# Layer 0's self attention: VectorE's order of minima and reciprocals, and its share of the copies of turned probabilities

## The reference

```python
scores = jnp.einsum('bhqd,bhkd->bhqk', Q, K) / dk ** 0.5
scores = jnp.where(causal, scores, -jnp.inf)
probs = jax.nn.softmax(scores, axis=-1)
attn = jnp.einsum('bhqk,bhkd->bhqd', probs, V)
```

## Time and profile before

| | |
|---|---|
| median of three runs | 858.41 us |
| the profiled execution | 859.32 us |
| its span | 857.4 us |
| TensorE busy | 767.4 us, 90% |
| VectorE busy | 612.8 us, 71% |
| ScalarE busy | 455.8 us, 53% |
| GpSimd busy | 432.6 us, 50% |
| L836 exponentials, ScalarE | 88.3 us busy, 192 instructions |
| L922 normalisation, GpSimd | 82.0 us busy, 80 instructions |
| L678 copies of turned probabilities, VectorE | 28.7 us busy, 48 instructions |

### The profile page before, as it was taken

The page is one execution under the profiler, slowest core; times in us unless marked ns, Lnnn a source line. Parts: engine busy times, 40 slices in busy tenths (PEclk is TensorE's granted clock), DMA queues, the critical chain, the costliest instruction groups (busy, mean ns, idle before and its releaser), DMA issues. The chain is left out here.

```text
span 857.4 us, 18273 instructions
## 1 busy us (share of the span) xinstructions
PE 767.4 (90%) x5842; PEld 483.8 (56%) x5842; DVE 612.8 (71%) x2052; ACT 455.8 (53%) x1447; POOL 432.6 (50%) x428
## 2 busy tenths in 40 slices
PE   6999989897959999999999999999894699999943
PEld 3766666665834444555555555787674555555523
DVE  1666777796856777898888888342345778888956
ACT  2387787673431001888888888100333087777724
POOL 4355565562004666766666666000630478888840
PEclk9999999999979999999999999999996599999977
DMA  9400000000004666300000000240378222222225
GB/s 323 189 2 2 2 2 1 2 1 1 1 14 101 166 171 152 99 2 2 1 1 1 2 1 1 109 206 18 107 260 211 104 63 76 75 79 72 73 64 190
DMA packets 32237, 63.17 MB, mean 74 GB/s; under 512 B 6592, under 2 KB 21068, under 8 KB 31280
## 3 DMA queue, kind: packets, MB, share of 16 engines
q1 hardware_dynamic: 20704, 41.40, 15.1%
q0 software_dynamic: 4896, 11.95, 4.5%
q10 hardware_dynamic: 6544, 8.67, 3.8%
HBM read 41.01 MB, written 9.84 MB: 59 GB/s over the span
## 5 line engine op out<-in xcount | busy, mean ns | idle before, releaser
L1418 ACT ACTIVATE a_room<-a_room,a_nm 128x257 f32<-128x257 f32 x256 | 127.3, 499 | 100.6 <-DVE a_nm L1261 99.8
L1460 POOL TENSOR_TENSOR a_room<-a_room,a_rd 128x1024 f32<-128x1024 f32 x64 | 121.3, 1895 | 65.8 <-DVE a_rd L1269 65.4
L1261 DVE CUSTOM_DVE_ANT_0 a_room<-a_ps,table,NSK 128x256 f32<-128x256 f32 x256 | 107.8, 478 | 0.4 <-PE a_ps L1120 0.4
L836 ACT ACTIVATE l_Pr<-l_Sm,l_nm 128x128 f32<-128x128 f32 (+1 forms) x192 | 88.3, 461 | 32.9 <-DVE l_nm L656 18.9
L922 POOL TENSOR_TENSOR l_Pr<-l_Pr,l_rd 128x256 f32<-128x256 f32 (+1 forms) x80 | 82.0, 1043 | 46.7 <-DVE l_rd L670 46.5
L1120 PEld LDWEIGHTS a_ps<-room 64*128 64x128 f32 x512 | 44.1, 186 | 53.2 <-issue 48.5
L1120 PE MATMUL a_ps<-room 64*128 64x256 f32 x512 | 72.3, 402 | 0.5 <-DVE a_nm L1261 0.5
L1200 PE MATMUL a_ps<-a_room,W 128*128 128x512 f32 x160 | 71.2, 602 | 0.8 <-ACT a_room L1432 0.8
L1241 DVE SCALAR_TENSOR_TENSOR a_room<-a_ps,BQK,table 128x512 f32<-128x512 f32 x80 | 56.4, 746 | 20.6 <-PE a_ps L1200 20.6
L1135 PE MATMUL a_ps<-table,a_room 128*128 128x128 f32 x512 | 69.7, 279 | 1.1 <-ACT a_room L1427 1.1
L1148 PE MATMUL a_psO<-a_room,room 128*64 128x512 f32 x256 | 68.8, 617 | 0.0
(11 more groups left out here) (323 smaller groups left out, 1780.6 us busy)
## 6 DMA issues: line engine op xcount, KB each, us to landing
room<-a_room SPq DMA_DIRECT2D x96, 64.0 KB, 2.0
room<-a_room ACTq DMA_DIRECT2D x96, 64.0 KB, 2.1
room<-in_w_in SPq DMA_DIRECT2D x1, 6144.0 KB, 18.3
room<-in_c_in SPq DMA_DIRECT2D x1, 4096.0 KB, 15.3
room<-pairs SPq DMA_DIRECT2D x8, 512.0 KB, 8.0
W<-in_w SPq DMA_DIRECT2D x1, 3072.0 KB, 12.4
room<-in_w_out SPq DMA_DIRECT2D x1, 3072.0 KB, 20.0
W<-in_wo SPq DMA_DIRECT2D x1, 2048.0 KB, 8.4
```

What stands on the lines that cost most here:

```text
L836: nc.scalar.activation(Pr[:, t % 4, n, 0:n_keys], Sm[:, t % 2, n, 0:n_keys], ACT.Exp, bias=nm[:, t % 2, n:n + 1], scale=-1.0, accum_out=de ...
L1261: nc.vector.tensor_tensor_reduce(out=Sm[:, t % 2, n, 0:S], in0=psS(t)[:, n // 2, n % 2, :], in1=c["window"][:, n % 2, :], scale=-1.0, scal ...
L1418: nc.scalar.activation(Pr[:, t % 4, n, :], Sm[:, t % 2, n, :], ACT.Exp, bias=nm[:, t % 2, n:n + 1], scale=-1.0, accum_out=den[:, t % 2, n: ...
L1460: pool.tensor_tensor(p, p, rd[:, t % 2, :].unsqueeze(2).to_broadcast([P, 4, S]), ALU.mult).then_inc(normed, 1)
```

## The change

In self slots VectorE now issues peak(t) before invert(t-1), as it did in cross slots. In odd self slots (16 of them) VectorE copies both banks of turned probabilities, one behind the other, after its single wait for both halves of the turn; ScalarE has no copy in these slots. The first of the two copies counts up `copied_a`, the second `copied_v`. The number and size of all copies stay the same. Cross slots and the rest of the program are not edited.

```diff
     def kind(self, t):
         return self.groups[t // 2][0]
+
+    def both_by_vector(self, t):
+        return self.kind(t) == "self" and t % 2 == 1
 
                 w = plan.width(t)
+                if plan.both_by_vector(t):
+                    nc.vector.tensor_copy(PT[:, i % 2, 2 * (t % 2), 0:w], psT[:, 0, 0:w]).then_inc(s["copied_a"], 1)
                 nc.vector.tensor_copy(PT[:, i % 2, 2 * (t % 2) + 1, 0:w], psT[:, 1, 0:w]).then_inc(s["copied_v"], 1)
 
             for t in range(steps):
-                if t < slots and plan.kind(t) == "cross":
+                if t < slots:
                     peak(t)
                 if 0 <= t - 1 < slots:
                     invert(t - 1)
-                if t < slots and plan.kind(t) == "self":
-                    peak(t)
 
                 if t < slots:
                     exps(t)
-                if 0 <= t - LT < slots:
+                if 0 <= t - LT < slots and not plan.both_by_vector(t - LT):
                     keep(t - LT)
```

## The result

The changed kernel takes 868.95 us (median of four runs, 866.44 to 872.1) against 858.58 (four runs of the kernel before): ratio 1.0102, interval 1.0078 to 1.0125. Slower, as forecast, but by 10.4 us between the medians and 8.7 between the profiled executions instead of 4.3, and outside the range (858.8 to 865.2). The profiled execution took 868.06 with a span of 866.3; before's span was 857.4, so 8.9 us are to be found.

A forecast was written before the change was run, and what follows sets the result against it. TensorE was taken to bound layer 0's attention. Batch terms +1.36, +1.13, +1.0 and +0.8 sum to +4.3 us on the profiled 859.32, giving 863.6, less 0.9 for the median: 862.7 us; 8-in-10 range 858.8 to 865.2.

The forecast's parts named there:

- The new ring from odd turn to odd turn: Layer 0 self slots: turn, two copies, minima, reciprocal, normalisation, next odd turn take 5.29 us; TensorE needs 4.93.
- +1.36 in the first batch: Layer 0, first batch: turn(2) at 55.06, then odd turns 5.29 apart bring turn(10) to 75.86 instead of 74.50.
- +0.70 at turn(13): Layer 0, behind the first output: double copy and later minima(14) put turn(13) at 87.06 instead of 86.36.
- The sign the prediction named: Start of layer 0's cross attention: the first cross score comes 3.5 to 4.3 us later than before.
- The delay stays: Behind layer 0: each stage takes its input from the last, so the +4.3 us reach the end unchanged.
- With the new order alone every ring would be of 4.81: Layer 0 self slots: with one copy per slot, rings take 4.81 us, below TensorE's 4.93 for two slots.
- TensorE's rate: Rival, layer 0 self slots: two slots stay at 4.93 us and only the cover moves; 857.8 us, chance 0.13.
- ScalarE's relief: Rival, layer 0 behind outputs: fewer ScalarE copies shorten the recovery; 853.1 us at best, 855 likelier, chance 0.05.
- the dearer pair: Rival, odd self slots: second copy held to the first's end, ring 5.45 us; 864.3 to 866 us, chance 0.14.
- No later stage took the delay in: Rival, stages behind layer 0: a wait ending at a fixed time absorbs the delay; 858.5 to 860 us, chance 0.06.

The follow-up runs named there:

- order_odd_steps: The changed kernel, but in even self steps the reciprocal stands ahead of the minima again; ratio 1.012 (1.008 to 1.016) to the kernel before.
- the badly filled one: The changed kernel with three extra matmuls in each of TensorE's two waits behind an output, which stood behind ScalarE's copy and waited 2.39 us; ratio 1.025.

## Why the prediction was right or wrong

- *The new ring from odd turn to odd turn, 5.29*: right, measured 5.21; every link within 0.05 of its row. The last was 0.05, not 0.10, and the pair of copies 0.94, not 0.96. order_odd_steps shows that the minima in it make the difference.
- *+1.36 in the first batch*: 1.1 (first scores to output 35.52 against 34.43), as three passes through the ring at 0.08 less give. The odd turns wait 0.22 for GpSimd, not 0.3 to 0.4.
- *Behind the outputs +0.70 at turn(13)*: 0.62 counted from the output (87.56 less 77.37 is 10.19, before 9.57), of which the wait before score 16 has 0.38 and that before turn 13 0.24. Both items over all batches: forecast 3.9 to the first cross scores, measured 3.1. Right in mechanism, 0.8 too much. The sign the prediction named, the first cross score 3.5 to 4.3 later, came at 3.1.
- *"The delay stays: behind layer 0 every stage takes its input from the last"*: this step failed. It let the delay pass through unchanged and so put the change of TensorE's clock at nothing; the earlier trace rows gave 1.00 and no reason why that should last. The runs showed half clock behind the longer waits, and later stages met more of it too: +6.3 us from the first cross scores on, where the forecast added about 0.4. Some 4.8 of these are the three further stretches at half clock. The same omission is in "With the new order alone every ring would be of 4.81", taken as harmless: the order alone, with 0.24 more of waiting in one place per batch, cost 0.9%.
- *The rivals*: TensorE's rate did not hold, ScalarE's relief gained nothing, and the second copy was not held to the end of the first (0.48 after 0.56), so the dearer pair is out as well. No later stage took the delay in. None of them named the clock. That the change would be slower was forecast from a mechanism that the trace shows; its size was not.
- *Supported by runs, not settled*, that two waits behind an output bring half clock when they are long enough: it shows between 43 and 155 us in all seven profiles in which both are there and add up to 1.33 us or more. These are the changed kernel three times and four others; the badly filled one is left aside. It shows in none of the eight in which they add up to 1.18 or one of them is gone or filled. By places, it followed 12 of the 21 outputs in the seven profiles and none of the 24 in the eight. So a longer wait makes it likely and not certain. The two sums were found after the runs and nothing between them was measured. Why the clock also falls in the feed-forward stays open: a stretch at half clock stands there (between 208 and 236 us) in 11 of the 14 profiles of kernels other than the one before, those with shorter waits in layer 0 too, and in neither of the kernel before. The waits are alike and the clock isn't; before, then after:

```profile
211.57 1.99 PE L530 MATMUL l_psS<-HAD,QT 128*128 128x256 f32 x8 [2.24 <-ACT QT L849]
213.40 1.04 PE L554 MATMUL l_psO<-KT,TU 128*128 128x256 bf16 x8
```

```profile
215.97 3.12 PE L533 MATMUL l_psS<-HAD,QT 128*128 128x256 f32 x8 [2.24 <-ACT QT L852]
218.88 1.64 PE L557 MATMUL l_psO<-KT,TU 128*128 128x256 bf16 x8
```

## What to carry to other kernels

When TensorE sets the pace, add up the rings that run through it, one copy or reduction at a time; a ring over two slots has to fit into TensorE's two slots, and a free average on the other engines does not help. Price an added TensorE wait with its clock: here 0.45 us added to a wait that was already there, three times, cost five times itself, and a saved wait gave nothing back when a later stage ran at the lower clock instead. Read the granted clock by stage in both kernels before any other cause is looked for.

## What the runs showed of the hardware that was not expected

Three copies of 0.48 us added to a kernel of 874.5 us cost 0.9%, and seven of the ten runs bore nearly all of it. A clock of 1.00 throughout a stage is no reserve: behind waits of 0.56 and 0.62 it held in two profiles, behind 0.47 and 0.86 it fell at one output of three. The Trainium skill, TensorE: Matmul & The Clock Gate, Part 1, says that the gate follows how busy TensorE has lately been and has two levels, 1.2 and 2.4 GHz; the 1.48 against 0.83 us of the same six matmuls goes the same way, at 1.8 times.
